# The attention projection of a four-stage residual kernel, computed for two items at once from fp32r halves

## What is computed

```python
attn_in = tanh(x @ W1 + b1)            # 512 -> 128 channels
scores  = attn_in @ v
p       = softmax(where(mask[kind], scores, -1e30))
x = x + (p @ x) / cnt                  # 1: attention pooling
h = relu(x @ w1[lang] + b1[lang])
a = x + h @ w2[lang] + b2[lang]
x = x + layernorm(a) * gamma[lang] + beta[lang]      # 2: adapter
x = x + zX * lap_x + zY * lap_y + zR * x * (1 - x)   # 3: reaction and diffusion
x = x + x @ W[cat] + b[cat]            # 4: category, 512 x 512 weights per item
```

## Time and profile before

| | |
|---|---|
| median of 3 runs | 1074.25 us (1072.41 to 1077.02) |
| the profiled execution | 1069.11 us |
| its span, first to last instruction | 1067.3 us |
| PE busy | 1047.7 us, 98% |
| DVE busy | 889.5 us, 83% |
| ACT busy | 500.9 us, 47% |
| POOL busy | 528.3 us, 49% |
| chain that ended last | PE 93% |

### The profile page before, as it was taken

The page is one execution under the profiler, slowest core; times in us unless marked ns, Lnnn a source line. Parts: engine busy times, 40 slices in busy tenths (PEclk is TensorE's granted clock), DMA queues, the critical chain, the costliest instruction groups (busy, mean ns, idle before and its releaser), DMA issues.

```text
span 1067.3 us, 22722 instructions
## 1 busy us (share of the span) xinstructions
PE 1047.7 (98%) x4912; PEld 653.2 (61%) x4912; DVE 889.5 (83%) x2090; ACT 500.9 (47%) x1422; POOL 528.3 (49%) x537
## 2 busy tenths in 40 slices
PE   6999999999999999999999999999999999999997
PEld 3666666666666666666666666666666666666663
DVE  5888888888888888888888888888888888888885
ACT  3544544444444444445445444444444444444442
POOL 3354455455455455445445444545544544544554
PEclk9999999999999999999999999999999999999999
DMA  8787897688878977776786868798888788887874
GB/s 330 237 273 222 259 303 238 210 264 253 260 232 280 326 259 238 235 232 203 236 273 198 251 227 264 249 295 248 245 269 265 241 257 262 267 286 234 262 231 163
DMA packets 119108, 268.82 MB, mean 252 GB/s; under 512 B 13010, under 2 KB 13028, under 8 KB 111556
## 3 DMA queue, kind: packets, MB, share of 16 engines
q1 hardware_dynamic: 63428, 166.24, 47.6%
q10 hardware_dynamic: 55552, 101.15, 31.2%
HBM read 243.21 MB, written 33.55 MB: 259 GB/s over the span
## 4 chain that ended last, share of the span: by engine, by line
PE 93%; issue 2%; DVE 1%; ACTq 1%; DMA 1%; POOL 1%; ACT 1%; SPq 0%; DVEq 0%; POOLq 0%
PE ps_out L423 40%; PE bank_hidden L378 10%; PE ps_attn L356 10%; PE ps_adapt L405 10%; PE ps_pool L396 10%; PE ps_x3T L413 5%; PE bank_scores L367 3%; PE bank_hidden L389 3%; PE bank_scores L384 1%; PE bank_scores L368 1%; ACTq L235 1%; DMA rows_near<-x 1%; POOL b_wide L895 0%; DMA col_rows<-in_cols 0%; DVE x L770 0%
## 5 line engine op out<-in xcount | busy, mean ns | idle before, releaser
L423 PE MATMUL ps_out<-w3s,x3T 128*128 x1024 | 501.9, 600 | 2.4 <-ACT x3T L485 2.4
L882 POOL TENSOR_TENSOR neighbours<-x 128x510 f32<-128x510 f32 x128 | 132.8, 1037 | 212.6 <-DVE x L747 212.6
L423 PEld LDWEIGHTS ps_out<-w3s,x3T 128*128 128x128 f32 x1024 | 165.5, 191 | 106.5 <-issue 105.1
L874 POOL TENSOR_TENSOR rstd<-var_eps,minus_half 128x1 f32<-128x1 f32 x128 | 70.4, 550 | 273.6 <-DVE var_eps L732 273.6
L888 POOL TENSOR_TENSOR rows_near<-rows_near 128x512 f32<-128x512 f32 x128 | 163.0, 1274 | 32.3 <-DMA rows_near<-x 32.0
L356 PEld LDWEIGHTS ps_attn<-xts,w_attn 128*128 128x128 f32 x1024 | 134.3, 191 | 61.2 <-issue 60.3
L541 ACT ACTIVATE attn<-ps_attn,vals 128x128 f32<-128x128 f32 x128 | 47.1, 368 | 255.1 <-issue 181.8
L895 POOL TENSOR_TENSOR b_wide<-b_wide,x 128x512 f32<-128x512 f32 x128 | 163.0, 1273 | 1.5 <-DMA b_wide<-in_b 1.5
L356 PE MATMUL ps_attn<-xts,w_attn 128*128 128x128 f32 x1024 | 135.1, 275 | 0.5 <-issue 0.5
L378 PE MATMUL bank_hidden<-w_all,xts 128*128 x1024 | 135.3, 275 | 0.0
L405 PE MATMUL ps_adapt<-w_all,hid 128*128 x256 | 131.3, 595 | 0.1
(11 more groups left out here) (111 smaller groups left out, 1283.4 us busy)
## 6 DMA issues: line engine op xcount, KB each, us to landing
w3s<-in_w SPq DMA_DIRECT2D x128, 1024.0 KB
rows_near<-x SPq DMA_DIRECT2D x256, 252.0 KB
xts<-in_xT ACTq DMA_DIRECT2D x128, 256.0 KB, 4.3
xs<-in_x ACTq DMA_DIRECT2D x128, 256.0 KB, 4.6
b_wide<-in_b ACTq DMA_DIRECT2D x128, 256.0 KB, 4.5
out_x<-res SPq DMA_DIRECT2D x128, 256.0 KB, 4.4
w_all<-in_w1l SPq DMA_DIRECT2D x1, 2560.0 KB, 8.9
w_all<-in_w2l SPq DMA_DIRECT2D x1, 2560.0 KB, 14.5
```

The lines of the kernel that those rows point to most:

```text
L423: mm = pe.matmul(ps_out[:, :], x3T[:, j.ring(2), k * P:(k + 1) * P], w3s[:, bass.ds(wslot * (K * D) + k * D, D)], start=(k == 0), stop=(k ...
L882: nc.gpsimd.tensor_tensor(neighbours[:, q, 1:D - 1], x2[:, q, 0:D - 2], x2[:, q, 2:D], ALU.add).then_inc(neighbours_ready, 1)
```

## The change

- `attn_project` runs once for a pair of items, in the even slots of PE. W1 and the transposed x are each split into a high and a low half of type float32r; three products (high-high, high-low, low-high) are summed, over 256 columns. That is 12 matmuls for a pair.
- W1 is split once at the start, by ACT and POOL. ACT writes the high half of x transposed (`split_high`(s+1), behind tanh), and POOL subtracts it for the low half (`split_low`(s+3), first in POOL's slot). The halves of items 0 and 1 are made ahead, the low ones by DVE. Both pairs of halves have one buffer, which the next pair overwrites once the projection is done.
- tanh runs once for a pair, over 256 columns, in ACT's odd slots.
- xT has a ring of four buffers and is loaded two items ahead; its buffer is free after `adapter_project` and `split_low`.
- To make room, `x1_b2` and `x1_beta` become single buffers, with waits on the square and on `normalize` of the item before; the square's output goes to `x1_b2`; `v_wide` is replaced by a broadcast column; tables of the start share memory with tiles of the loop, and the first `load_w3` waits for the split of W1.

```diff
+            def attn_project(p):
+                pe.wait_ge(hi_ready, 2 * p.upto())
+                pe.wait_ge(lo_ready, 2 * p.upto())
+                if p.is_first:
+                    pe.wait_ge(w1a_lo_made, 1)
+                if p.is_at_least(1):
+                    pe.wait_ge(attn_ready, p.upto(1))
                 for k in range(K):
-                    mm = pe.matmul(ps_attn, w1_attn[:, k * A:(k + 1) * A], xts[:, r, k, :],
-                                   start=(k == 0), stop=(k == K - 1))
+                    part = slice(k * A, (k + 1) * A)
+                    pe.matmul(ps_attn, w1_attn_hi[:, part], xts_hi[:, k].rearrange("p i s -> p (i s)"),
+                              start=(k == 0), stop=False)
+                    pe.matmul(ps_attn, w1_attn_hi[:, part], xts_lo[:, k].rearrange("p i s -> p (i s)"),
+                              start=False, stop=False)
+                    mm = pe.matmul(ps_attn, w1_attn_lo[:, part], xts_hi[:, k].rearrange("p i s -> p (i s)"),
+                                   start=False, stop=(k == K - 1))
                 mm.then_inc(attn_mm, 1)
...
             def slot(s):
                 if s.inside(B):
                     words[(s).n] = load_params(pe, LANG, 2, s)
-                    attn_project(s)
+                if s.inside(B) and s.ring(2) == 0:
+                    attn_project(Step(s.n // 2))
...
+            def split_high(t):
+                act.wait_ge(xT_in[t.ring(4)], t.dma(4))
+                if t.is_at_least(2):
+                    act.wait_ge(attn_mm, t.n // 2)
+                nc.scalar.activation(xts_hi[:, :, t.ring(2)], xts[:, t.ring(4)], ACT.Copy).then_inc(hi_ready, 1)
...
-                if (s - 1).inside(B):
-                    attn_tanh(s - 1)
+                if (s - 1).inside(B) and (s - 1).ring(2) == 0:
+                    attn_tanh(Step((s - 1).n // 2))
+                if (s + 1).inside(B) and not s.is_first:
+                    split_high(s + 1)
                 if (s - 3).inside(B):
                     variance(s - 3)
...
+            for t in range(2):
+                dve.wait_ge(hi_ready, t + 1)
+                nc.vector.tensor_tensor(xts_lo[:, :, t], xts[:, t], xts_hi[:, :, t].bitcast(F32), ALU.subtract
+                                        ).then_inc(lo_ready, 1)
...
             def add_b2(s, lang):
...
+                if s.is_at_least(1):
+                    dve.wait_ge(y_ready, s.upto(1))
+                    dve.wait_ge(var_ready, s.upto(1))
...
             def add_beta(s, lang):
...
+                if s.is_at_least(1):
+                    dve.wait_ge(x2_ready, s.upto(1))
...
+            def split_low(t):
+                pool.wait_ge(hi_ready, t.upto())
+                nc.gpsimd.tensor_tensor(xts_lo[:, :, t.ring(2)], xts[:, t.ring(4)],
+                                        xts_hi[:, :, t.ring(2)].bitcast(F32), ALU.subtract).then_inc(lo_ready, 1)
...
             def slot(s):
+                if s.is_first:
+                    split_low(s + 2)
+                if (s + 3).inside(B):
+                    split_low(s + 3)
                 if s.inside(B):
                     inverse_std(s)
                     sum_columns(s)
```

More of the change, by code:

```diff
@@ L6 @@
 F32 = mybir.dt.float32
+F32R = mybir.dt.float32r
 BF16 = mybir.dt.bfloat16
@@ L148, in cond_residual_kernel @@
         hid = sb("hid", [P, 2, S])
-        x1_b2 = sb("x1_b2", [P, 2, D])
-        x1_beta = sb("x1_beta", [P, 2, D])
+        x1_b2 = sb("x1_b2", [P, D])
+        x1_beta = sb("x1_beta", [P, D])
         y_sum = sb("y_sum", [P, 2])
         neg_mean = sb("neg_mean", [P, 2])
-        square_junk = sb("square_junk", [P, D])
         var_sum = sb("var_sum", [P, 2])
@@ L163, in cond_residual_kernel @@
         res = sb("res", [P, 2, D])
-        ps_attn = pb("ps_attn")[:, 0:S]
+        lang_rows = res[0:3 * ROWS, 0]
+        kind_parts = x3[:, 0, 0:3 * B]
+        ids_rows, col_rows, ones_row = neighbours[0:NID, 0, 0:B], neighbours[0:NCOL, 0, B:B + P], neighbours[0:1, 0, 2 * P:3 * P]
+        iota_row = neighbours[:, 0, 3 * P:4 * P]
+        ps_attn = pb("ps_attn")[:, 0:2 * S]
         bank_scores = pb("bank_scores")
@@ L366, in attn_scores @@
                     pe.wait_ge(mixT_ready, b.upto(1))
-                pe.matmul(ps_scores, v_wide[:, :], attn[:, b.ring(2), :], start=True, stop=False)
+                pe.matmul(ps_scores, vals[:, V:V + 1].broadcast_to([A, P]), attn[:, b.ring(2), :], start=True, stop=False)
                 pe.matmul(ps_scores, ident16[:, :], masks16[:, bass.ds(kind * P, P)], start=False, stop=True
@@ L371, in adapter_project @@
             def adapter_project(s, lang):
-                pe.wait_ge(xT_in[s.ring(3)], s.dma(3))
+                pe.wait_ge(xT_in[s.ring(4)], s.dma(4))
                 if s.is_first:
@@ L377, in adapter_project @@
                 for k in range(K):
-                    mm = pe.matmul(ps_xw, xts[:, s.ring(3), k, :], w1_all[:, bass.ds(lang * (K * A) + k * A, A)],
+                    mm = pe.matmul(ps_xw, xts[:, s.ring(4), k, :], w1_all[:, bass.ds(lang * (K * A) + k * A, A)],
                                    start=(k == 0), stop=(k == K - 1))
@@ L552, in load_xT @@
             def load_xT(a, item):
[L553 to L556, removed]
+                r = a.ring(4)
+                if a.is_at_least(4):
+                    act.wait_ge(xw_mm, a.upto(4))
+                    act.wait_ge(lo_ready, a.upto(4))
                 act.dma_start(xts[:, r], xT[bass.ds(item, 1)].rearrange("o p (k s) -> p (o k) s", k=K)
@@ L746, in normalize @@
                 dve.wait_ge(rstd_ready, h.upto())
-                nc.vector.scalar_tensor_tensor(x2[:, q, :], normed[:, :], rstd[:, q:q + 1], x1_beta[:, q, :],
+                nc.vector.scalar_tensor_tensor(x2[:, q, :], normed[:, :], rstd[:, q:q + 1], x1_beta[:, :],
                                                ALU.mult, ALU.add).then_inc(x2_ready, 1)
@@ L776, in add_b2 @@
                     dve.wait_ge(b2_moved, L)
-                nc.vector.tensor_tensor(x1_b2[:, s.ring(2), :], ps_pool[:, :], b2_wide[:, bass.ds(lang * D, D)],
+                if s.is_at_least(1):
+                    dve.wait_ge(y_ready, s.upto(1))
+                    dve.wait_ge(var_ready, s.upto(1))
+                nc.vector.tensor_tensor(x1_b2[:, :], ps_pool[:, :], b2_wide[:, bass.ds(lang * D, D)],
                                         ALU.add).then_inc(x1_b2_ready, 1)
@@ L782, in add_beta @@
                     dve.wait_ge(beta_moved, L)
-                nc.vector.tensor_tensor(x1_beta[:, s.ring(2), :], ps_pool[:, :], beta_wide[:, bass.ds(lang * D, D)],
+                if s.is_at_least(1):
+                    dve.wait_ge(x2_ready, s.upto(1))
+                nc.vector.tensor_tensor(x1_beta[:, :], ps_pool[:, :], beta_wide[:, bass.ds(lang * D, D)],
                                         ALU.add).then_inc(x1_beta_ready, 1)
```

70 lines of the change are left out of this document (36 added, 34 removed).

## The result

| | before | changed |
|---|---|---|
| median of 4 runs | 1074.01 us | 1382.68 us (1374.31 to 1407.26) |
| ratio to before | | 1.2876, 95% interval 1.2844 to 1.2908 |
| profiled execution, its span | 1069.11, 1067.3 | 1379.19, 1377.4 |
| mean granted clock | 1.000 | 0.923 |

Slower by 309 us, 29%. That is the forecast direction, by the loop that was forecast, but it is 113 us over the forecast 1270 and outside the range. One of the four runs, 1407.26, was slow; the median of the other three is 1379.19, and comparisons with the experiments go by that.

What follows compares the result with a forecast made beforehand. TensorE, 98% busy, was taken to bound the kernel before; the change adds a four-engine wait loop. 1069.1 + 193 (loop) + 2 (start) + 3 (jitter) = 1267, rounded to 1270 against the median; range 1195 to 1360.

Steps and rivals of the forecast that it cites:

- the loop that was forecast: Wait closing through four engines once per pair: 19.09 us for two items against 16.08, 193 us over 64 pairs; chance 0.79.
- its place decides: GpSimd's low half queues behind b3, so the pair's projection waits for the end of GpSimd's queue; PE idle some 3.5 per pair.
- the chain of four engines: From projection through PE, ScalarE, VectorE and GpSimd to the low half the next projection wants: 19.09 us per pair.
- ScalarE's odd split: On ScalarE, the odd item's high-half split stands ahead of the square, inside the loop, at 0.57 us.
- The single buffers: Single x1_b2 and x1_beta on VectorE cost nothing, as epsilon and normalize already cover the waits.
- third rival: TensorE's clock falls in the stalls: 2 us longer per pair, 1270 + 128 = 1398; chance 0.06.
- the middle of two items: ScalarE's stretch from the mix to the place of tanh, taken as 2.30, between 2.09 and 2.50.
- 0.05 a pair for jitter: Loop jitter from ScalarE's parameter stretch, 2.09 to 3.16, put at 0.05 a pair, 3 us in all.
- The fp32r price: On PE, an fp32r matmul of 256 columns takes 0.11 us, so twelve take 1.32 per pair.
- the bf16 row's 0.11: Lower bound for a 256-column fp32r matmul on PE, from bf16 spreads of 512 columns 0.22 apart; the price taken.
- the transpose's 0.22: Price for 256 columns at the f32 transpose's pace: twelve matmuls 2.64, 84 us more, 1355; chance of fp32r slower 0.08.
- The rival in which the low halves are in time: No stall, PE stays the bound, only the matmuls' 0.46 per pair counts: 1074 - 29 + 2 = 1047; chance 0.06.

Runs made afterwards that it cites:

- e1: Changed kernel with GpSimd's low half moved from its slot's head to behind rstd, one item further ahead: 1087.65 us, ratio 1.0171.
- e9: Changed kernel with the low half, of item s+4, between rows and b3 instead of at the next slot's head: 1285.71 us, ratio 1.2008.
- e5: Changed kernel with 24 filler matmuls ahead of each projection from the third pair and ScalarE's high half behind the square: 1271.78 us, ratio 1.1877.
- e10: Kernel before with only the single x1_b2 and x1_beta, their waits, and the square's output in x1_b2: 1070.82 us, ratio 0.9996.
- e7: Changed kernel with 12 filler bf16 matmuls ahead of each projection from the third pair: 1340.05 us, ratio 1.2508.
- e2: Changed kernel with 24 filler bf16 matmuls ahead of each projection from the third pair: 1306.81 us, ratio 1.2201.
- e6: Changed kernel with the low half behind rstd, one item further ahead, and the high half behind the square: 1068.07 us, ratio 0.9982.
- e8: As e6, with 12 filler matmuls once, ahead of the first projection: 1066.60 us, ratio 0.9953.
- e3: Changed kernel with ScalarE's high half moved from ahead of the square to behind it, no fillers: 1377.05 us, ratio 1.2870.

## Why the prediction was right and wrong

**Right: what makes the kernel slow.** The step "its place decides" holds in each part. The low half follows b3 at once, and waits for ScalarE only twice, 9.7 us in all. The projection waits for it and not for the high half: 59 + 3 waits in the rows for 64 pairs, 3.28 in the timeline where the prediction had 2.4 to 3.9 (and "some 3.5"). Moving that one instruction removed the stall (e1), and taking one instruction of 1.24 out ahead of it made the wait 1.2 shorter (e9).

**Right: the chain of four engines.** The prediction put ScalarE's odd split, 0.57, inside the loop; e5 took it out and gained 0.54 per pair. The single buffers, put at nothing, cost nothing (e10).

**Wrong: the clock was left to a rival.** This is the step that failed. The sum priced all of PE's links after the stall at the 2.4 GHz level. The prediction had the mechanism as its third rival, at 2 us a pair and a chance of 0.06, although the loop itself forecast idle stretches of 3.5 us, 64 times, such as the loop of before never has. It argued only that no such gap was there to read; that is a reason for not knowing, not for 0.06. Measured: 1.28 a pair, 77 us, the bulk of the miss. It isn't the rival's 2 because the clock falls after most stalls, 47 of 60, and not after all. Where it falls, it costs 1.2 to 1.7 mostly and 2.9 in ten pairs. The Trainium skill (TensorE: Matmul & The Clock Gate, Why this matters for your kernels) warns of idle gaps between bursts of matmuls; the trace agrees, and e7 shows that waits of 1.9 us still cost 33 us against e2.

**Wrong: the addition.** The terms of the loop, as the prediction lists them, add up to 19.39 and not to 19.09. With 0.30 more for each of 64 pairs the same text would have forecast 1289.

**Wrong in size: two links of the loop.** All links can be read from the timelines; means over 60 pairs, us:

| from, to | forecast | e2 | changed |
|---|---|---|---|
| projection, adapter_up | 7.61 | 7.80 | 9.16 |
| adapter_up, mix | 0.80 | 0.80 | 0.80 |
| mix, split | 2.30 | 2.51 | 2.43 |
| split, square | 0.57 | 0.54 | 0.54 |
| square, epsilon | 0.81 | 0.80 | 0.80 |
| epsilon, normalize | 1.69 | 1.69 | 1.69 |
| normalize, b3 | 3.05 | 3.06 | 3.06 |
| b3, low half | 1.24 | 1.23 | 1.22 |
| low half, next projection | 1.32 | 1.37 | 1.36 |
| sum | 19.39 | 19.8 | 21.1 |

In e2 the first row is longer by the projection alone: 1.51 instead of 1.32, a first step of 0.20 and eleven of 0.12. In the changed kernel the same row holds the clock's cost, 1.36, of which a slightly shorter stretch returned 0.08. The stretch between mix and split is ScalarE's load of its parameters: in 59 of 60 pairs of both kernels it is that load's own length, 0.73 to 2.99, plus 0.69. The sum took the middle of two items for it, and had 0.05 a pair for jitter.

**The whole account.** The changed period is 4.94 over the one before (21.07 less 16.13), the forecast one was 3.06 (3.01 and 0.05 for jitter). Of the 1.88 between them the clock is 1.28, the addition 0.30, the links 0.35 (0.40 less the 0.05 put down for jitter); the kernel before gives back 0.05, as its period is 16.13 and not 16.08. Over 60 pairs that is 113 us, and the profiled execution missed its forecast of 1267 by 112. The start and the last pair together cost what the forecast had for them, within 1 us: the first projection starts 2.6 later (24.26) and the fourth pair 13.9 later, where the forecast gives 2 and three periods of 3.06 more, 11.2; the forecast has one more such 3.06 for the last pair, but from its projection to the end it is 44.3 us, and 44.6 before. In e2, 41 over 1267 by its profiled execution, the loop is 36, start and end are 5.

**The fp32r price** was right in kind: the bf16 row's 0.11 was the near bound, the transpose's 0.22 the far one, and the runs show 0.12. The saving of 0.46 a pair is 0.38 at the floor (16.08 less 15.7). Of that e6 keeps 0.14 in its period (15.99 against 16.13), some 9 us in all, and its fourth pair starts 8 us late. e8 ends 4 us under the kernel before.

**The other side.** The rival in which the low halves are in time never came up in the changed kernel; it took an edit to GpSimd's order to get there, and to ScalarE's, and then gave 1068 and not 1047, since the late start and the periods above the floor remain.

## What to carry to other kernels

A helper step on an idle engine is not free because the engine is idle: ask in which slot its result is wanted, what stands ahead of it in that engine's program, and when that ends. Here GpSimd had half its time free, and the place of 1.27 us of work made 292 of 309 us. If a change creates idle stretches on TensorE again and again, price the work behind them at both clock levels, and take that case into the likeliest sum. And compare two such variants with the clock held up (fillers did it), or the clock can hide what the edit did. Last, add the terms of a sum up once more, and check its links one by one against the new trace.

## What the runs showed of the hardware that was not expected

- Matmuls that compute nothing, put into a wait, made the kernel faster: 24 of them per pair, 1379 to 1307 us, the mean granted clock 0.923 to 0.993.
- After a stall of 3.3 us the clock stood at 0.50 for some 6 us at full work (721 to 727), and it can fall after PE has resumed, in the middle of a run of matmuls (699.96). Most falls cost about half as much as the one at 721: 1.2 to 1.7 us in 37 of 60 pairs, 2.9 in 10.
- The length of the wait alone doesn't fix the clock: the changed kernel's waits are 3.28 nearly every time, and 13 of 60 cost no clock; e3's have a mean of 3.08, and only 2 of 60 cost none. Waits of 1.9 us behind 12 fillers gave 0.964, bare waits of 2.1 gave 0.945.
- ScalarE's parameter load, from SBUF into registers, takes 0.70 to 2.99 us in the changed kernel, and its length passes into the loop one to one (min, median and max in ns):

```profile
L240 ACTq TENSOR_LOAD <-all_params x128: 698/1557/2986, 13.6 to 1308.3; - x128
```

- The fp32r matmul of 256 columns steps by 0.12 us at the full clock and by 0.21 at the low one. ScalarE's write of 128x512 as fp32r takes 625 ns (its plain copy of x3T out of PSUM 591), GpSimd's subtraction to fp32r 1268, as its plain fp32 b3 (1269):

```profile
L920 POOL TENSOR_TENSOR xts_lo<-xts,xts_hi 128x512 fp32r<-128x512 f32 x126 | 159.8, 1268 | 9.7 <-ACT xts_hi L554 9.7
...
L554 ACT ACTIVATE xts_hi<-xts 128x512 fp32r<-128x512 f32 x128 | 80.0, 625 | 124.9 <-issue 65.9
```
